# B and C of a Mamba scan spread over the partitions by transfers instead of by selection matmuls

## What is computed

```python
x_dbl = jnp.einsum('hod,blhd->blho', xw, xh)
dt_r, Bm, Cm = jnp.split(x_dbl, [H_DT, H_DT + H_DS], axis=-1)
...
def step(s, inp):
    d_t, u_t, B_t, C_t = inp
    dA = jnp.exp(d_t[..., None] * A)
    s = s * dA + (d_t * u_t)[..., None] * B_t[:, :, None, :]
    y_t = jnp.einsum('bhdn,bhn->bhd', s, C_t)
    return (s, y_t)
```

## Time and profile before

| | |
|---|---|
| median of 3 runs | 1313.71 us (1312.18 to 1315.65) |
| the profiled execution | 1312.99 us, its span 1311.1 us |
| TensorE busy | 1052.0 us (80%) |
| VectorE busy | 1113.3 us (85%) |
| ScalarE busy | 803.8 us (61%) |
| GpSimd busy | 864.6 us (66%) |
| granted TensorE clock, mean | 0.902 |

### The profile page before, as it was taken

One profiled execution on the slowest core, in us unless ns is written; L12 is line 12 of the kernel. 1 busy time (PEld: TensorE's weight loads), 2 busy tenths in 40 slices (PEclk: granted clock), 3 DMA queues, 4 the chain that ended last, 5 costly groups with the idle time before them and its releaser, 6 DMA issues.

```text
span 1311.1 us, 15848 instructions
## 1 busy us (share of the span) xinstructions
PE 1052.0 (80%) x3949; PEld 523.5 (40%) x3949; DVE 1113.3 (85%) x1364; ACT 803.8 (61%) x1245; POOL 864.6 (66%) x708
## 2 busy tenths in 40 slices
PE   0766568889889989889899988887888878788775
PEld 0432234545444454545445453343333333343322
DVE  7658879797887979798896979999998989999996
ACT  3574357676676866666675766656575666656521
POOL 2327887575665757576575758677776868686755
PEclk9987779999999999999999999879887979878766
DMA  6512122121113121120212112111212121210211
GB/s 148 151 45 66 44 86 66 40 73 40 47 26 80 32 71 42 40 72 7 74 32 80 32 40 57 27 42 29 57 40 52 44 49 48 48 48 0 61 43 42
DMA packets 62905, 69.62 MB, mean 53 GB/s; under 512 B 11488, under 2 KB 49280, under 8 KB 62848
## 3 DMA queue, kind: packets, MB, share of 16 engines
q1 hardware_dynamic: 58752, 60.65, 18.6%
q0 software_dynamic: 4096, 8.40, 2.1%
HBM read 18.69 MB, written 16.78 MB: 27 GB/s over the span
## 4 chain that ended last, share of the span: by engine, by line
POOL 37%; issue 29%; PE 18%; DVE 6%; SPq 3%; DMA 3%; ACT 3%; POOLq 1%; DVEq 0%; ACTq 0%
POOL s_sb L565 24%; POOL expert_in L572 4%; POOL xn L543 4%; POOL dd L523 3%; DMA dsp<-dd 3%; DVE u_sb L909 2%; PE bank L1126 2%; PE bank L1225 2%; DVE s_sb L982 2%; PE bank L1192 2%; POOL dd L533 2%; PE bank L1185 2%; PE bank L1203 2%; PE bank L1210 2%; SPq L396 1%
## 5 line engine op out<-in xcount | busy, mean ns | idle before, releaser
L565 POOL TENSOR_TENSOR s_sb<-s_sb,c_of 128x512 f32<-128x512 f32 x480 | 628.6, 1312 | 344.9 <-DVE s_sb L982 339.1
L982 DVE TENSOR_TENSOR_SCAN s_sb<-bank,u_sb 128x512 f32<-128x512 f32 x512 | 619.1, 1209 | 0.0
L760 ACT ACTIVATE bank<-bank,a_neg 128x510 f32<-128x510 f32 x512 | 336.5, 661 | 260.5 <-PE bank L1210 244.9
L909 DVE TENSOR_TENSOR u_sb<-bank,b_of 128x512 f32<-128x512 f32 x512 | 345.5, 675 | 143.0 <-PE bank L1203 132.1
L1203 PE MATMUL bank<-dsp,sel_d 128*128 128x512 f32 x512 | 329.2, 643 | 47.3 <-DMA dsp<-dd 23.2
L1210 PE MATMUL bank<-dsp,sel_d 128*128 128x512 f32 x512 | 241.2, 471 | 71.6 <-DVE s_sb L982 68.4
L1203 PEld LDWEIGHTS bank<-dsp,sel_d 128*128 128x128 f32 x512 | 107.0, 209 | 198.2 <-DVE u_sb L909 111.0
L1210 PEld LDWEIGHTS bank<-dsp,sel_d 128*128 128x128 f32 x512 | 107.5, 210 | 193.8 <-DVE s_sb L982 152.8
L1225 PE MATMUL bank<-s_sb,con 128*32 128x512 f32 x1024 | 152.8, 672 | 13.2 <-POOL s_sb L565 9.3
L1126 PE MATMUL bank<-xnT,wx 128*128 (+1 forms) x256 | 129.7, 601 | 0.0
L1159 PE MATMUL bank<-bc,sel_bc 128*128 128x512 f32 x128 | 60.2, 522 | 43.5 <-ACT b_of L721 26.4
(11 more groups left out here) (146 smaller groups left out, 1225.3 us busy)
## 6 DMA issues: line engine op xcount, KB each, us to landing
dsp<-hi SPq DMA_DIRECT2D x64, 256.0 KB
dsp<-dd SPq DMA_DIRECT2D x64, 256.0 KB
expert_in<-dd SPq DMA_DIRECT2D x8, 512.0 KB, 6.5
xn<-expert_in SPq DMA_DIRECT2D x8, 512.0 KB, 4.3
xn<-L_ffn_W SPq DMA_DIRECT2D x16, 256.0 KB, 4.5
expert_out<-xn SPq DMA_DIRECT2D x16, 256.0 KB, 2.5
out<-acc SPq DMA_DIRECT2D x8, 512.0 KB, 5.2
expert_in<-xn,put_at POOLq DMA_INDIRECT x64
```

Source lines behind the costliest of these rows:

```text
L565: pool.tensor_tensor(s_now, s_now, c_of[:, hf, hh, :], ALU.mult).then_inc(S["p_ready"], 1)
L760: act.activation(d, d, ACT.Exp, scale=a_neg[:, k:k + 1]).then_inc(S["decay_ready"], 1)
L909: dve.tensor_tensor(u_sb[:, w % U_RING, :], du_ps[w % 2][:, :], b_of[:, hf, head_of(w), :], ALU.mult).then_inc(S["u_ready"], 1)
L982: dve.tensor_tensor_scan(s_sb[:, w % S_RING, :], decay_of(w)[:, :], u_sb[:, w % U_RING, :], 0.0, ALU.mult, ALU.add).then_inc(S["scan_done" ...
```

## The change

`bc` is now made once (64 rows, `bcw` has 64 columns) and stays in full 32-bit. ScalarE copies it (`take_bc`, two slots after TensorE made it), and SP repeats it over the partitions: for each half four transfers from 16 partitions of `bc` to 128 of `b_of` or `c_of`, 256 KB each. They are issued when the last product that reads the old B and C of that half is done: product 15 for the next chunk's first half, product 31 of the chunk before for the second. So that `bc` is filled by then, GpSimd waits for `take_bc` ahead of products 15 and 31; `take_bc` waits until the four transfers before have landed. `bc_low`, `spread_bc` on TensorE, `copy_bc` and the matrix `sel_bc` are gone, and 8 of the 16 small weight loads for `bcw`.

The tables move: D1 from slot 2 to 0, z0 from 3 to 1, x0 from 4, 5, 6, 7 to 2, 4, 5, 7, and the last four steps of the softplus one slot earlier.

```diff
-STAGE_A = {"z0": (3,), "x0": (4, 5, 6, 7), "bc0": (8,), "v0": (11,), ...
-           "D0": (18,), "B0": (23,), "B1": (23,), "C0": (23,), "C1": (23,), "bc1": (25,), "v1": (26,)}
+STAGE_A = {"z0": (1,), "x0": (2, 4, 5, 7), "bc0": (8,), "v0": (11,), ...
-D_1 = (2,)
+D_1 = (0,)
-SOFTPLUS = {"act": (2, 3, 4, 5), "scale": (10,), "zero": (11,), "low": (14,), "high": (14,)}
+SOFTPLUS = {"act": (2, 3, 4, 5), "scale": (9,), "zero": (10,), "low": (13,), "high": (13,)}
...
+            def spread_bc(ch, hf):
+                if ch[0] == 0:
+                    sp.wait_ge(*tile_read((-1, None), f"bc{hf}"))
+                else:
+                    wait_products(sp, *((ch, 0) if hf else (before(ch), UNITS)))
+                for k, (kind, of) in enumerate((("b", b_of), ("c", c_of))):
+                    for hh in range(2):
+                        r0 = (k * 2 + hh) * NS
+                        sp.dma_start(of[:, hf, hh, :], bc[r0:r0 + NS, :].unsqueeze(1).broadcast_to([NS, UC, CH])
+                                     ).then_inc(S[f"{kind}_loaded{hf}"], 16)
...
+                        if w % UNITS == UNITS - 1 and ch[0] + 1 < CHUNKS:
+                            pool.wait_ge(*tile_read(ch, f"bc{w // UNITS}"))
...
+            def take_bc(ch, hf, src):
+                name = f"bc{hf}"
+                if ch[0] > 0 or hf > 0:
+                    of = ch if hf else before(ch)
+                    for kind in "bc":
+                        act.wait_ge(*bc_loaded(of, 1 - hf, kind))
+                act.wait_ge(S["misc_pe"], tile_made(src, name))
+                act.activation(bc[0:4 * NS, :], tile_bank(src, name)[0:4 * NS, :], ACT.Copy).then_inc(S["misc_bc"], 1)
```

More of the change, by code:

```diff
@@ L226, in read_slot @@
             slots, _, by = next(x for x in plan if x[1] == name)
-            return slots[-1] + (READ_ACT if by in ("act", "copy") else READ_DVE)
+            return slots[-1] + (READ_ACT if by in ("act", "bc") else READ_DVE)
         def softplus_slots(hf):
@@ L708, in split_high @@
                 act.activation(hi, dd, ACT.Copy).then_inc(S["hi_ready"], 1)
-            def copy_bc(ch, src, kind, hf):
-                if kind == "B":
-                    wait(act, "u_ready", per_chunk(ch, SLOTS, UNITS * (hf - 1)))
-                elif hf == 0 and ch[0] > 0:
-                    wait_products(act, before(ch), UNITS)
-                elif ch[0] > 0:
-                    wait_products(act, ch, 0)
-                for hh in range(2):
-                    name = f"{kind}{2 * hf + hh}"
-                    act.wait_ge(S["misc_pe"], tile_made(src, name))
-                    act.activation((b_of if kind == "B" else c_of)[:, hf, hh, :], tile_bank(src, name)[:, :],
-                                   ACT.Copy).then_inc(S["misc_copy"], 1)
             def expert_copy(ch, th):
@@ L738, in _ @@
             silus(first, 0, start)
-            bc_high(first, 0, start)
+            take_bc(first, 0, start)
             for step in softplus_before(0, "act"):
@@ L743, in _ @@
             take_delta(first, 0)
-            copy_bc(first, start, "B", 0)
-            copy_bc(first, start, "C", 0)
             split_high(first, 0)
-            bc_high(first, 1, start)
+            take_bc(first, 1, start)
             for step in softplus_before(1, "act"):
@@ L778, in body @@
                             softplus_start(after(ch), hf_, ch, 0)
-                        elif by == "copy" and hf_ % 2:
-                            copy_bc(after(ch) if hf_ < 2 else ch, ch, name[0], hf_ // 2)
                         elif name[:2] == "xt":
@@ L944, in _ @@
             first, start = (0, None), (-1, None)
-            bc_low(first, 0, start)
             dve.wait_ge(S["route_pe"], 1)
@@ L964, in _ @@
             dve.tensor_copy(put_at[:, :], r_t).then_inc(S["routed"], 1)
-            first, start = (0, None), (-1, None)
-            bc_low(first, 1, start)
             spread_u(first, 0)
@@ L1245, in _ @@
             delta(first, start, "D0")
-            for name in ("B0", "B1", "C0", "C1"):
-                spread_bc(first, start, name)
             x_proj(first, start, "bc1")
```

99 lines of the change are left out of this document (39 added, 60 removed).

## The result

The changed kernel takes 1234.29 us (median of 4 runs, 1233.74 to 1234.84); the kernel before took 1314.08 us beside it (4 runs, 1312.18 to 1315.65). The ratio is 0.939 with a 95% interval from 0.938 to 0.941. The profiled execution has a span of 1232.9 us, 78.2 less than before.

A forecast was written before the change was run, and what follows sets the result against it. The prediction took VectorE as the path, losing time where TensorE has too much between two units. Experts' chunks 46, gathering chunks 14 and start and end 0: 1312.99 − 46 − 14 − 0 = 1253 us, range 1238 to 1288.

The forecast's parts named there:

- the estimate of 7.2: New transfers: a 1 MB stack lands 7.2 us after its first issue, the nearest row for a set of four.
- the head of the experts' stretch: Experts' chunks, TensorE from slot 23: spread of B and C, with 2.02 us standing for a bank; o0 3.3 us earlier without it.
- The late transfers: Rival, 5%: 1 MB lands in 29 us, holding ScalarE's exponentials in slots 10 and 27; 165 us, 1418 us.
- 5.8 forecast: Gain per expert's chunk, 4.5 + 0.8 + 0.4 + 0.1; eight of them 46 us.
- 4.5 + 0.8 + 0.4 = 5.7: Expert's chunk gains: 4.5 in slots 23 to 31, 0.8 from D1's gap, 0.4 from the silu gap in slot 9.
- the 0.1 forecast: Expert's chunk: removing `bc_low` gains only 0.1 us, as one precedes a gap and the other a wait for outp.
- the 0.84 of the prediction: Time of one `bc_low` on VectorE: 0.73 us to the next multiplication plus 0.1 hand-over from ScalarE.
- 2.3 forecast: Gain per gathering chunk: 1.7 from `bc_low`, 0.6 from the gap in slot 24, nothing from D1; six chunks 14 us.
- 1.7 forecast: Gathering chunk: `bc_low` removed from nearly full VectorE, 0.84 us twice a chunk.
- Its price for D1: Expert's chunk, slots 0 to 11: the gap of 1.40 us shrinks to about 0.6 with D1 moved, gaining 0.8.
- TensorE cools: Rival, 10%: earlier D1 meets 1.2 GHz, taking 6.9 us for 3.4; 1273 us if in six gathering chunks, 1301 in all fourteen.
- Start and end, 0 forecast: Start, chunks 0 and 15: gains of 1.1 and 0.8 against 1.5 us lost to D1 in chunk 0; together 0, between −2 and +2.

## Why the prediction was off

- **Direction and path: right.** VectorE gained where TensorE had stood, and no engine waits for one of the new transfers in the steady chunks. A set of four is 1.05 MB, and its last bytes are moved at 571.5, 8.5 us after its first issue at 563.0, beside the estimate of 7.2. What the path gained by was only half as told: the 2.02 us at the head of the experts' stretch, which the prediction calls the spread, stood behind ScalarE's rounding too, and either half of the change alone takes most of it away. The late transfers (1418 us) did not come.
- **Experts' chunks, 5.8 forecast, 7.0 measured.** Grouped over seven chunks: VectorE's gaps ahead of the multiplication fell from 76.8 to 46.0 us and those ahead of the expert's output from 13.0 to 10.4, 4.8 a chunk together; the prediction's 4.5 + 0.8 + 0.4 = 5.7 are the same things and somewhat too much, since the gap behind h11 did not shrink with the rest. `bc_low` took 1.4 of VectorE's time a chunk, and put back alone it costs 0.8, in place of the 0.1 forecast. This is the step that failed in these chunks: I gave it nothing because the one stood in front of a gap and the other in front of a wait for outp. But the gap left behind it is set by TensorE's blocks after it (2.31 before, 2.60 now), so it hides only 0.3, and there is no wait for outp for the other to hide, with TensorE standing 0.9 us in place of 1.3 for the silu that comes before outp. Another 0.4 is VectorE's product of the gate (12.3 to 9.8 us in seven chunks), which is the term below. 4.8 + 1.4 + 0.4 are 6.6 of the 7.0; the hand-overs around `bc_low` would be 0.3 of the rest, if each adds the 0.15 by which the 0.84 of the prediction exceeds its 0.69.
- **Gathering chunks, 2.3 forecast, 3.9 measured.** This step failed too: the missing term is VectorE's own instructions becoming shorter. Per chunk, over the five periods from chunk 10 to 15, which are 4.2 us shorter each: the product of the gate 13.1 to 7.7 us in five chunks (1.1), the low part 17.6 to 12.5 (1.0), the combine steps 16.0 to 13.2 (0.6): 2.7 us. `bc_low` gave 1.4 (1.7 forecast), TensorE's gaps 0.5 (0.6), and add_out now waits 0.5 for outp. In the period from 9 to 10, which gained only 2.7, a single combine step of the changed kernel takes 3.07 us where the others take 0.32. The rows were there before: the forecast read the gaps and took the busy time of instructions that the change does not touch as fixed.
- **The moved slots.** The prediction gave them 0.8 + 0.4 in an expert's chunk and 0 in a gathering one, 10 us; they are worth 47 with the transfers and 25 without. Its price for D1 (1.40 to 0.6, measured 0.30) was small but sound. What it lacked is who waits for what these steps release: the relu of h03 and the silu behind ScalarE's rounding, TensorE in slot 14 for the stack, which stood on the chain of the earlier trace rows, and who meets whom on VectorE and GpSimd.
- **TensorE cools: it would have.** With the transfers and the old slots, D1's first two pieces in a gathering chunk take 2.08 us in place of 1.02 and VectorE's gap behind it is 3.05, twice that of before. With D1 in slot 0 it starts at the full clock, right behind two late units and the sum. The rival had its mechanism right and its place wrong.
- **Start and end, 0 forecast.** Neither of the two terms came as forecast: D1's gap in chunk 0 is 0.45, where I had 1.5, and the stack of chunk 1 is 3.7 us earlier, of which 1.8 are its slot.

The sum: 60 + 8 x 1.2 + 6 x 1.6 = 79, against 80 measured.

Left open: of the 39 us of the softplus steps 18 are the low part and 4 the rounding; the other 16 (the product with x and the zeroing a slot later) were not taken apart. In that kernel TensorE stands 3.4 us for the silu of a gathering chunk (before 1.4, changed 1.5), and ScalarE's rounding ahead of the silu waits 3.2 us for GpSimd's zeroing (changed 2.5), so the chain is in the rows, but no run has it alone. The parts need not add up either, since the waits of the kernel with all four steps late are not those of the two kernels that move one or two.

## What to carry to other kernels

Removing work next to a hand-written order is worth what it removes plus what the order can then do, and the second can be the larger part: ask of each moved step not only what it waits for but who waits for what it releases. Where TensorE and ScalarE share banks, price a tile by its hand-over and not by its matmul or its copy, which were free here one by one. And in a stretch where VectorE is nearly full, look at how long the same instruction takes at its different places: the spread between the shortest and the longest is time that a shift by one slot gives or takes.
